# Attention on one Trainium2 core: the values' product in four tiles of 32 columns, and reciprocals spread by ScalarE instead of by DMA

## The reference

```python
q = (x @ Wq).reshape(B, N, H, Dh).transpose(0, 2, 1, 3)      # 4 x 16 heads x 1024 x 64
s = jnp.einsum('bhid,bhjd->bhij', q * scale, k)
gm = jnp.max(s, axis=-1, keepdims=True)                      # over all keys, masked ones too
p = jnp.where(causal_mask, 0.0, jnp.exp(s - gm))
num = jnp.einsum('bhij,bhjd->bhid', p, v)
out = num / (jnp.sum(p, axis=-1, keepdims=True) + EPS)
return out.transpose(0, 2, 1, 3).reshape(B, N, H * Dh) @ Wo + bo
```

## Time and profile before

| | |
|---|---|
| median of 3 runs | 1795.34 us (1795.25 to 1795.99) |
| the profiled execution: its own time | 1796.03 us |
| its span, first to last instruction | 1794.30 us |
| mean granted TensorE clock | 0.981 |
| attention | from 0 to about 1240 us |
| PE busy | 1703.6 us (95%) |
| POOL busy | 1310.6 us (73%) |
| DVE busy | 1318.2 us (73%) |
| ACT busy | 1007.0 us (56%) |

### The profile page before, as it was taken

The page is one execution under the profiler, slowest core; times in us unless marked ns, Lnnn a source line. Parts: engine busy times, 40 slices in busy tenths (PEclk is TensorE's granted clock), DMA queues, the critical chain, the costliest instruction groups (busy, mean ns, idle before and its releaser), DMA issues. The chain is left out here.

```text
span 1794.3 us, 32641 instructions
## 1 busy us (share of the span) xinstructions
PE 1703.6 (95%) x11638; PEld 1233.6 (69%) x11638; DVE 1318.2 (73%) x2395; ACT 1007.0 (56%) x2145; POOL 1310.6 (73%) x1354
## 2 busy tenths in 40 slices
PE   6999999999999999999999999985999979889998
PEld 4767676776767767676766776654888755568786
DVE  6767766776767776677766777643999958979887
ACT  2555444455454545444544445442989876649876
POOL 1778677776877767777776777774899957738998
PEclk9999999999999999999999999996999989989999
DMA  3000000000000000000000000111000000000000
GB/s 96 2 13 13 19 19 13 13 13 25 13 13 13 17 20 13 13 13 24 13 13 12 13 24 13 36 26 42 1 1 1 1 1 1 1 1 7 13 13 18
DMA packets 27377, 27.67 MB, mean 15 GB/s; under 512 B 4529, under 2 KB 18642, under 8 KB 27218
## 3 DMA queue, kind: packets, MB, share of 16 engines
q1 hardware_dynamic: 27218, 25.59, 5.4%
HBM read 6.70 MB, written 2.10 MB: 5 GB/s over the span
## 5 line engine op out<-in xcount | busy, mean ns | idle before, releaser
L1183 DVE TENSOR_REDUCE attn_neg<-attn_shared 128x2 f32<-128x1024 f32 x512 | 611.9, 1223 | 305.6 <-PE attn_shared L1365 304.1
L1046 ACT ACTIVATE attn_prob<-attn_shared 128x1024 f32<-128x1024 f32 x288 | 295.4, 1027 | 374.7 <-PE attn_shared L1392 374.5
L949 POOL TENSOR_TENSOR attn_row_sum<-attn_row_sum,attn_prob 128x1024 f32<-128x1024 f32 (+3 forms) x256 | 417.4, 1630 | 24.5 <-POOL attn_row_sum L949 0.4
L312 ACT ACTIVATE experts_weighed<-experts_y,kept_gate 128x128 f32<-128x128 f32 x1024 | 279.5, 412 | 49.2 <-PE experts_y L559 41.5
L926 POOL TENSOR_TENSOR attn_prob<-attn_prob,attn_below 128x256 f32<-128x256 f32 x256 | 189.7, 741 | 130.9 <-ACT attn_prob L1046 130.8
L405 DVE SCALAR_TENSOR_TENSOR experts_acc<-experts_y,kept_gate,experts_acc 128x128 f32<-128x128 f32 x896 | 247.0, 342 | 22.7 <-PE experts_y L559 20.3
L1361 PE MATMUL attn_shared<-attn_qk_hi 64*128 64x512 f32 x1024 | 228.0, 429 | 8.4 <-DVE attn_neg L1183 3.5
L557 PE MATMUL experts_y<-kept_w_hi,kept_xT_hi 128*128 128x512 f32 x512 | 206.0, 402 | 3.8 <-PEq L725 1.8
L558 PE MATMUL experts_y<-kept_w_lo,kept_xT_hi 128*128 128x512 f32 x512 | 201.8, 394 | 0.0
L559 PE MATMUL experts_y<-kept_w_hi,kept_xT_lo 128*128 128x512 f32 x512 | 201.4, 393 | 0.0
L965 POOL TENSOR_TENSOR attn_o_norm<-attn_o,attn_den 128x512 f32<-128x512 f32 x64 | 81.3, 1292 | 137.5 <-DMA attn_den<-attn_sums_of 137.5
(11 more groups left out here) (272 smaller groups left out, 3550.9 us busy)
## 6 DMA issues: line engine op xcount, KB each, us to landing
attn_den<-attn_sums_of SPq DMA_DIRECT2D x256, 64.0 KB, 2.0
kept_x<-in_L_attn_a_x_dram SPq DMA_DIRECT2D x4, 512.0 KB, 8.3
kept_half_raw<-_ffn_expert_weights_dram SPq DMA_DIRECT2D x4, 512.0 KB, 5.2
out_dram<-kept_x SPq DMA_DIRECT2D x8, 256.0 KB, 2.3
attn_prob<-in_L_attn_a_Wkv_dram SPq DMA_DIRECT2D x2, 512.0 KB, 5.9
attn_prob<-in_L_attn_a_Wq_dram SPq DMA_DIRECT2D x1, 512.0 KB, 4.8
attn_wo<-in_L_attn_a_Wo_dram SPq DMA_DIRECT2D x1, 512.0 KB, 5.7
attn_bo<-in_L_attn_a_bo_dram SPq DMA_DIRECT2D x1, 64.0 KB, 5.8
```

Source lines behind the costliest of these rows:

```text
L312: ins = act.activation(weighed[n][:, e, :], y[fill(pair, quad, odd) % RING][:, e * D:(e + 1) * D], ACT.Copy, scale=k.gate[:, c, quad * PER ...
L949: pool.tensor_tensor(row_sums(p, n)[:, :, at:], row_sums(p, n)[:, :, at:], src, ALU.add).then_inc(add_ok, 1)
L1046: act.activation(prob[n % RING][:, :, :], buffer((p, t))[:, :, :], ACT.Exp).then_inc(exp_ok, 1)
L1183: dve.tensor_reduce(neg[p % 2][:, :, b, half], buffer((p, b, half))[:, :, :], AX.X, ALU.max, negate=True).then_inc(max_ok, 1)
```

## The change

Five things change.

- `product`: four matmuls in 128x32 tiles for each part in place of two in 128x64 tiles. A head's 64 value columns are taken as two sets of 32 (`two`), and the rows of `pv`, and so of `o`, `o_norm` and `wo`, are in the order (set, head, column). `wo` is loaded by four DMAs in that order.
- `spread`: the DMAs are gone. With the new order both heads of a half lie in adjacent quadrants, as in `sums`: sums of head h in half n are in quadrant 2h + n as before, and three ACT copies of 64 rows bring them to the right rows: two copies of rows 64 to 127 of `den[0]` to the lower and upper half of `den[1]`, then, after a wait for both, one of rows 0 to 63 to rows 64 to 127. `sums_of` is gone: `denominator` writes to `den[0]`, for which it waits until `normal` of the round before has read it. The copies stand in ACT's list in step 1 of round p+1, ahead of `product_out(p+1, 0)`.
- `o[1]` has two buffers, and `product_out` waits for `norm_ok` of two rounds before.
- On POOL both `normal` stand behind the masks and additions of the step.
- Last round: `sums`, `denominator`, `inverse` and `normal` are done by halves. The sums of the half that is complete after part 7 (n = 0) are taken directly after part 7, into all four quadrants, so that nothing needs to be spread; they go to a free `o_norm` buffer (`den_last`).

The core of the diff:

```diff
-                for h in range(2):
-                    cols = slice((2 * (p % 2) + h) * DH, (2 * (p % 2) + h + 1) * DH)
-                    ins = pe.matmul(pv[head(h), first:], v[g % 2][:, j, cols], slot(p, part)[:, h, place_of(part)],
-                                    start=(j == 0), stop=(i in (7, 11)))
+                for two in range(2):
+                    for h in range(2):
+                        at = (2 * (p % 2) + h) * DH + two * QUADRANT
+                        ins = pe.matmul(pv[quadrant(h, two), first:], v[g % 2][:, j, at:at + QUADRANT],
+                                        slot(p, part)[:, h, place_of(part)], start=(j == 0), stop=(i in (7, 11)))
...
-            def sums(p):
...
+            def sums(p, n):
+
+                alone_free(("sum", p, n))
+                if p == END:
+                    pe.wait_ge(add_ok, ADDS * END + (ADDS if n else 7))
+                    for h in range(2):
+                        for two in range(2):
+                            ins = pe.matmul(alone[quadrant(h, two), :], ones[:, :], row_sums(p, n)[:, h, :], start=True, stop=True)
...
                 if valid(r):
                     for i in range(3, 8):
                         product(r, i)
+                    if r == END:
+                        sums(END, 0)
...
-                need(act, norm_ok, 2 * p if n else 2 * (p - 2) + 1)
+                need(act, norm_ok, 2 * (p - 2) + n + 1)
...
-            def denominator(p):
-                act.wait_ge(sum_ok, p + 1)
-                need(act, spread_ok, SPREADS * 16 * p)
-                act.activation(sums_of[:, :], alone[:, :], ACT.Identity, bias=sum_eps[:, :], scale=1.0).then_inc(den_ok, 1)
+            def denominator(p, n):
+                act.wait_ge(sum_ok, sums_done(p, n))
+                if (p, n) == (END, 0):
+                    act.wait_ge(out_ok, END // 2)
+                if (p, n) != (END, 0):
+                    need(act, norm_ok, 2 * p)
+                to = den[0] if p < END else inverse_of(p, n)
+                act.activation(to[:, :], alone[:, :], ACT.Identity, bias=sum_eps[:, :], scale=1.0).then_inc(den_ok, 1)
+
+            def spread(p):
+
+                act.wait_ge(inv_ok, PIECES * (p + 1))
+                for two in range(2):
+                    act.activation(den[1][rows_of(two), :], den[0][rows_of(1), :], ACT.Copy).then_inc(moved_ok, 1)
+                act.wait_ge(moved_ok, 2 * (p + 1))
+                act.activation(den[0][rows_of(1), :], den[0][rows_of(0), :], ACT.Copy).then_inc(spread_ok, 1)
...
-                    if t == 0 and valid(r - 2):
-                        normal(r - 2, 0)
-                        normal(r - 2, 1)
+                    if r == END + 2 and t == 0:
+                        normal(END, 1)
...
+                    if t == 0 and r < END + 2 and valid(r - 2):
+                        normal(r - 2, 0)
+                        normal(r - 2, 1)
+                    if (r, t) == (END + 1, 1):
+                        normal(END, 0)
...
-                    if t == 1 and valid(r - 1):
+                    if t == 1 and valid(r - 1) or (r, t) == (END + 1, 0):
                         for piece in range(PIECES):
-                            inverse(r - 1, piece)
+                            inverse(r - 1, t, piece)
```

More of the change, by code:

```diff
@@ L623, in attention @@
     QUADRANT = 32
-    SPREADS = 8
     FIRST, LAST = -2, ROUNDS + 2
@@ L718, in attention @@
         if valid(r - 1):
-            single.append(("sum", r - 1, 0))
+            single.append(("sum", r - 1, 1))
         if valid(r + 1):
             single.append(("turned", r + 1, 0))
+        if r == END:
+            single.append(("sum", END, 0))
     place = {u: n for n, u in enumerate(shared)}
@@ L813, in row_sums, with quadrant, rows_of, sums_done @@
             return row_sum[n][p % len(row_sum[n])]
-        def quadrant(h, n):
-            return slice(QUADRANT * (2 * h + n), QUADRANT * (2 * h + n + 1))
+        def quadrant(h, two):
+            return slice(QUADRANT * (2 * two + h), QUADRANT * (2 * two + h + 1))
+        def rows_of(two):
+            return slice(two * DH, (two + 1) * DH)
+        def sums_done(p, n):
+            return p + 1 + (p == END and n)
+        def inverse_of(p, n):
+            return den_last if (p, n) == (END, 0) else den[n]
         def product_of(p, n):
@@ L852, in _ @@
                 sync.dma_start(k.half_raw[:, 8 * q:8 * q + 8, :], expert_w[8 * q:8 * q + 8].rearrange("e h d -> h e d")).then_inc(next_in, 16)
-            for p in range(ROUNDS - 3, ROUNDS - 1):
-                spread(p)
             sync.wait_ge(w_split, 2)
@@ L1116, in _ @@
                             high(r + 2, 1)
+                        if valid(r - 1) and r - 1 < END:
+                            spread(r - 1)
                         if valid(r):
                             product_out(r, 0)
+                        if r == END:
+                            denominator(END, 0)
                         if r == END:
@@ L1407, in product @@
                     pe.wait_ge(exp_ok, tile_count(p, i))
[L1408 to L1420 removed]
+                for two in range(2):
[3 more added lines that the diff above has]
+                                        slot(p, part)[:, h, place_of(part)], start=(j == 0), stop=(i in (7, 11)))
+                ins.then_inc(pv_ok, 1)
+            def sums(p, n):
+                alone_free(("sum", p, n))
+                if p == END:
+                    pe.wait_ge(add_ok, ADDS * END + (ADDS if n else 7))
+                    for h in range(2):
+                        for two in range(2):
+                            ins = pe.matmul(alone[quadrant(h, two), :], ones[:, :], row_sums(p, n)[:, h, :], start=True, stop=True)
+                else:
+                    pe.wait_ge(add_ok, ADDS * (p + 1))
+                    for h in range(2):
+                        for half in range(2):
+                            ins = pe.matmul(alone[quadrant(h, half), :], ones[:, :], row_sums(p, half)[:, h, :], start=True, stop=True)
                 ins.then_inc(sum_ok, 1)
```

50 lines of the change are left out of this document (20 added, 30 removed).

## The result

| | before | after |
|---|---|---|
| median | 1795.3 us (4 runs, 1792.72 to 1795.99) | 1783.43 us (4 runs, 1783.22 to 1784.67) |
| profiled execution, its own time | 1796.03 us | 1783.59 us |
| span | 1794.3 us | 1781.9 us |
| mean granted clock | 0.981 | 0.985 |

The ratio of the times is 0.9938 (95% interval 0.9921 to 0.9955): 11.9 us less, where 15.0 were forecast. The direction and the range (1774 to 1788) hold; 3.1 us of the gain are missing.

The account below looks back on a forecast made before the run. TensorE's own list was taken to bound 30 rounds, the open chain of factors the last stretch. 1796.03 - 5.3 (ordinary rounds) - 9.7 (last round) = 1781.0, minus 0.69 to the median: 1780.3 us; range 1774 to 1788 for 8 in 10.

Parts of the forecast that it names:

- Step 1: TensorE in ordinary rounds: groups of four tiles stay at 0.43 us, only the ends gain, 5.3 us together.
- The rival of slower tiles: Four tiles slower than two on TensorE, weight loads exposed by 0.03 us per group: 23 us more, 1803 us; chance 0.06.
- The estimate of 38 us: The skill's 60 cycles per matmul, paid in sequence for 1536 more TensorE records; the rival with a similar time had chance 0.03.
- Step 2(a): `denominator` on ACT now waits for both POOL products; 0.9 us left before the exponential in round 16, so cost nothing.
- 0.5 us in all 30 rounds: Rival: `denominator`'s wait for `normal` comes out late in ordinary rounds and takes back 15 us, 1795 us; chance 0.05.
- Step 2(b): The three ACT copies, from 663.2 to about 664.9 us in round 16, fit in idle time: cost nothing.
- (c): 256 DMAs of 64 KB go; nobody but POOL waited for them before round 30: nothing.
- Step 3: The last round's chain followed across the engines: gain 10.8 us, or 8.7 if the clock falls; 9.7 taken.
- the second variant: Last round with TensorE's clock at the lower level after a stop, `outwards(14)` 6.19 us instead of 3.82: gain 8.7 us.
- the middle that I took (9.7): Last round's gain in us, taken between 10.8 and the 8.7 with the lower clock.
- The rival "the last round gains little": The chain of the router and the experts' weights holds the last round, which gains nothing or little: 1790 us; chance 0.04.

Follow-up runs that it names:

- table early: The changed kernel plus a one-column exponential on ACT ahead of the waiting denominators' copy in rounds with a square root: 1780.52 us, 0.9930 of before.
- products first: The changed kernel with POOL's two products back at the start of step 0: 1772.87 us, 0.9889 of before; run again, 1770.68 us, 0.9881.
- the second batch: The changed kernel and the version with POOL's products in front, rerun beside the kernel before (1794.12 us): 1780.63 and 1770.68 us.
- last round whole: The changed kernel without the halves of the last round, its sums, copies and products done as in other rounds: 1790.66 us, 0.9988 of before.
- copies doubled: The changed kernel with two more 64-row ACT copies per round into a buffer nobody reads: 1785.76 us, 0.9964 of before.

## Why the prediction was right, and where it was not

**Step 1, right.** Groups of four at 0.43 us, no change of form between sums and product, 5.3 us. By itself it gave 4.72 us in 29 rounds (0.163 a round) and 4.4 us of the median. The rival of slower tiles is dead, and with it, as a price for this case, the rule of the Trainium skill ("TensorEngine Tiling (Array Packing)", section Instruction Overhead) of some 60 cycles for each matmul: there are 1536 further records, and a group of four lasts as long as one of two. The estimate of 38 us took each record for a matmul; with the two records of one matmul as one it would be 19 us, and the trace agrees with neither.

**Step 2(a), the step that failed.** "That leaves 0.9 us, so I cost it at nothing": true of round 16 (0.80 us measured). "In odd rounds ... it is no tighter there": wrong in five of them. I had listed as queued behind `denominator` on ACT the exponential, and not the table load that goes with it after a square root, though the trace of before has its row. 0.49 us in each of five rounds, 2.45 us; the early table gave back 2.17, products first 2.21. It was on the list of rivals only as 0.5 us in all 30 rounds. This is the 2.6 us by which e(1) to e(30) fell short (2.29 against 4.9), but for the 0.2 us by which Step 1 itself stayed under its 4.9.

**Step 2(b) and (c), right.** The copies cost 2.0 us where 1.7 was taken, and are hidden, with 0.8 us to spare; no DMA was missed.

**Step 3, right in its chain, off by the clock.** On the clock of the prediction (2.71 added) the exponentials of round 31 start at 1182.5 (1182.5 forecast), `denominator(30)` ends at 1199.35 (1199.2), the first mask of step 1 is at 1202.3 (1202.4), the last addition ends at 1215.1 (1214.9). Then TensorE runs at the lower clock, as the second variant had it, and sooner than I had thought: the eight matmuls for the router ahead of `outwards(14)` took 1.72 us, and 0.91 at the full clock with products first. `outwards(14)` starts at 1206.3 (1204.5 forecast) and takes 5.88 us in place of 3.82, 3.9 us late at its end where the variant had allowed 2. Of these, 1.6 us came back: `outwards(15)` runs from 1224.1 in place of 1221.1 and ends in 5.44 us where 5.9 were counted, and `x` is done at 1230.8 where the variant gave 1230.6. That it agrees to 0.2 us is in part luck. So the gain is 8.54 us, the variant's 8.7, and the middle that I took (9.7) was the mis-sized term, by 1.2 us. The rival "the last round gains little" is not borne out.

What the steps of the sum didn't say is how its parts weigh. The halves are worth 6.4 us, and all else together 2.15. Of this the second buffer gave 0.6 us by itself and the four tiles 0.9; if these add, 0.7 us is left for the DMAs and the order on POOL together, and this part holds a loss. I had computed 1199.2 for `denominator(30)` and entered it as a fact, without asking what it would be with the products first: 6.0 us earlier there, and 6.35 us at the end. Most of what the DMAs gave back had been spent on waits that the same change put in.

**The sum.** 5.3 + 9.7 = 15.0 forecast; 2.6 missing in the rounds by the table's load, 1.6 in the last two (the clock's 1.2, and 0.4 of Step 1 that lay outside the 29 rounds and is not seen there); 0.4 won at the start, and 1.2 in the experts, whose part varies by 5 us with the granted clock; 12.4 in the profiled pair, 11.9 between the medians, and 13.5 between those of the second batch.

Left open: how much of the 6.35 us is the clock alone. In the profiled executions of the changed kernel (two) and of "table early" TensorE stopped for 3.98 or 3.99 us ahead of the router's bank and then ran at the lower level, in those of "last round whole" and "copies doubled" it did so behind 2.4 us, and in neither of the two with products first did it stop or slow down at that place. 4.3 us of the 7.5 are there in POOL's additions already, which run without a gap from the first mask on. The other 3.2 us are POOL's wait for the router and the subtraction behind it; this wait hangs on TensorE's work at the lower clock and on the order of the products alike; these two were not separated.

## What to carry to other kernels

When an instruction is to wait longer, list all that its engine does up to the next thing that somebody waits for, in every kind of round, table loads included: the margin of one round (0.8 us) is not that of the five with a load of 1.28 us in it. Where a chain stands in the open at the end of a stage, ask of each new wait in it what the end would be without it; here the order of two instructions on POOL, with the clock that went with it, was worth 6.35 us, half of the change's own gain again. And a long stop of the busiest engine is worth what the next chain leaves of it: 4.3 of 5.58 us of stop taken away were worth 0.6.

## What the runs showed of the hardware

- A copy of 64 rows x 512 from one half of the partitions to the other took 0.64 us on ACT (1.28 for two), and the copy of 128 rows of the same length that moves the product out of PSUM 0.60. Half the rows were no cheaper; but only the second of the two reads PSUM, so the number of rows is not the only difference.
- A load of ACT's table took 1.28 us. It stood directly ahead of the exponential, behind a copy that waited for another engine (round 17 above), and a small exponential ahead of that copy moved it into the wait.
- The granted clock fell behind the stop of 3.99 us: 0.55 from 1199 to 1209 us of the changed kernel; with products first, without that stop, 1.00 from 1186 to 1205. The length of a stop alone did not decide it: behind a stop of 1.91 us at 1178.14 the first execution of products first had a clock of 0.50 from 1179.4 to 1182.8, and behind the same stop its second execution stayed at 1.00.
- The experts' part, the same work in every kernel, took 550.1 to 555.1 us in ten profiled executions, the shorter ones with less time at the lower clock level. A difference of a few us in a span is not told from it unless the marks are read.
